# The experts' output biases: from TensorE products to VectorE additions in the node layers

## The reference, cut to what matters

```python
def _L0_ffn_ref(x, Wr, br, W1, b1, ..., Wo, bo):
    ...
    w = jax.nn.softmax(feat @ Wr + br, axis=-1)          # one weight for each node and expert
    h = relu(_bn(einsum('bfd,edh->bfeh', x, W1) + b1))
    h = relu(_bn(einsum('bfeh,ehk->bfek', h, W2) + b2))
    y = jnp.einsum('bfeh,ehd->bfed', h, Wo) + bo         # bo: 8 x 256
    return jnp.einsum('bfed,fe->bfd', y, w)
x = x + _L0_ffn_ref(...)
```

## Time and profile before

| | value |
|---|---|
| median of three runs | 3030.54 us (3022.13 to 3033.51) |
| profiled execution, its own time | 3018.11 us |
| its span, first to last instruction | 3016.4 us |
| PE busy | 2650.0 us (88%) |
| DVE busy | 2043.3 us (68%) |
| ACT busy | 1400.9 us (46%) |
| POOL busy | 1054.2 us (35%) |
| mean granted TensorE clock | 0.948 of full speed |

### The profile page before, as it was taken

How to read it: one execution, slowest core, us unless ns; L and a number is a source line. 1 busy time by engine, 2 the same in 40 slices (tenths; PEclk the granted TensorE clock), 3 DMA queues, 4 the chain that set the end, 5 groups by cost and what they waited for, 6 DMA issues and landing times. The chain is left out here.

```text
span 3016.4 us, 54982 instructions
## 1 busy us (share of the span) xinstructions
PE 2650.0 (88%) x12024; PEld 2076.0 (69%) x12025; DVE 2043.3 (68%) x4092; ACT 1400.9 (46%) x2972; POOL 1054.2 (35%) x1184
## 2 busy tenths in 40 slices
PE   8777787779994999999999999999979977869698
PEld 6545555466552777777768888888858866647587
DVE  6686778868888454553227888888899959955411
ACT  3324332129881443443324444444388948845122
POOL 1676777722110000000006666666500008800043
PEclk9997999989996999999999999999989989989799
DMA  4798999937773000000017777777600131042353
GB/s 163 245 312 272 294 312 303 322 82 229 229 226 134 1 1 9 9 1 9 9 66 227 216 214 214 215 214 214 184 27 33 47 136 50 1 178 88 100 175 127
DMA packets 236592, 443.80 MB, mean 147 GB/s; under 512 B 29017, under 2 KB 128801, under 8 KB 235068
## 3 DMA queue, kind: packets, MB, share of 16 engines
q1 hardware_dynamic: 179518, 261.89, 27.8%
q0 software_dynamic: 56960, 180.47, 19.1%
HBM read 350.56 MB, written 92.69 MB: 147 GB/s over the span
## 5 line engine op out<-in xcount | busy, mean ns | idle before, releaser
L1912 PE MATMUL bank<-sums 128*128 128x256 f32 x2352 | 542.5, 381 | 2.6 <-issue 2.6
L1988 POOL DMA_INDIRECT conv_h<-table_h,conv_ix x392 | 374.2, 955 | 293.2 <-ACT conv_ix L1959 171.6
L1912 PEld LDWEIGHTS bank<-sums 128*128 128x128 f32 x2352 | 434.9, 191 | 54.9 <-issue 3.0
L1719 ACT ACTIVATE area<-bank,nodes_bi,nodes_sc 128x320 f32<-128x320 f32 x320 | 197.5, 617 | 347.2 <-PE bank L1627 347.2
L725 POOL DMA_INDIRECT x<-table_qv,scores_ix x300 | 283.9, 946 | 181.0 <-ACT scores_ix L626 102.7
L1890 DVE SCALAR_TENSOR_TENSOR x<-bank,nodes_w,x 128x256 f32<-128x256 f32 x200 | 96.4, 483 | 296.9 <-PE bank L1636 296.7
L1447 PE MATMUL bank<-attend_pv,x 128*128 128x260 f32 x800 | 220.4, 404 | 26.7 <-POOL attend_pv L1377 24.6
L745 PE MATMUL bank<-sums,area 128*128 x800 | 230.1, 416 | 11.0 <-issue 6.2
L1447 PEld LDWEIGHTS bank<-attend_pv,x 128*128 128x128 f32 x800 | 137.6, 191 | 109.4 <-issue 62.8
L1959 ACT ACTIVATE conv_ix<-src 128x2 int32 x196 | 39.9, 204 | 359.2 <-DVE conv_msg L2009 347.0
L2009 DVE TENSOR_TENSOR conv_msg<-bank,conv_h 128x512 f32<-128x512 f32 x196 | 135.5, 692 | 90.8 <-PE bank L1912 81.4
(11 more groups left out here) (490 smaller groups left out, 5764.6 us busy)
## 6 DMA issues: line engine op xcount, KB each, us to landing
sums<-in_edges SPq DMA_DIRECT2D x196, 384.0 KB, 3.2
x<-edge_v SPq DMA_DIRECT2D x200, 256.0 KB, 3.0
edge_v<-x SPq DMA_DIRECT2D x150, 256.0 KB, 4.7
hidden_rows<-top_wide SPq DMA_DIRECT2D x25, 512.0 KB, 3.4
projected<-spline_hst SPq DMA_DIRECT2D x10, 960.0 KB, 4.4
ball_hT<-projected SPq DMA_DIRECT2D x5, 1920.0 KB, 18.3
top_wd<-in_top_wd SPq DMA_DIRECT2D x8, 1024.0 KB
x<-in_x SPq DMA_DIRECT2D x10, 640.0 KB, 8.8
```

The source lines that it names most:

```text
L1719: nc.scalar.activation((h1, h2)[layer][:, o, hf * CW:(hf + 1) * CW], banks[n % HIDS][:, 0:CW], ACT.Relu, scale=sc[:, layer, e, o:o + 1], b ...
L1912: mm = nc.tensor.matmul(banks[u][:, g * F:(g + 1) * F], m.conv_eT[:, u, g, c], m.conv_w[:, c], start=False, stop=c == EC - 1, skip_group_c ...
L1988: nc.gpsimd.indirect_dma_start(out=h[:, u, g, :], out_offset=None, in_=m.d_h, in_offset=bass.IndirectOffsetOnAxis(ap=ix[:, u * G + g:u * G ...
```

## The change

The bias sum is taken from PE and ACT. The bias rows are loaded onto all 128 partitions in two tiles of 4 x 256 (0.5 MB each), instead of one of 8 x 256. VectorE adds w[k] times bias row k itself: after the sums of expert 0 it does k = 0, after expert 2 k = 1, after 4 k = 2 and 3, after 5 k = 4 and 5, after 6 k = 6 and 7, each with five instructions of 128 x 256. The two PE pieces, ACT's copies, the wait for them and the three additions behind expert 7 go. The semaphore `biased` now counts single additions, and DVE waits on it where the same x is touched next.

```diff
-        bo = st.sb("bo", [XQ, F])
+        near_bo = st.sb("bo", [P, few, F])
+        far_bo = flat[:, NP + 3 * U * F:NP + 3 * U * F + few * F].rearrange("p (e f) -> p e f", f=F)
+        bo = [near_bo[:, e] for e in range(few)] + [far_bo[:, e] for e in range(few)]
+        biases_after = {0: (0, 1), 2: (1, 2), 4: (2, 4), 5: (4, 6), 6: (6, XQ)}
...
-        wT = st.sb("wT", [XQ, CH])
...
                     for k, x in enumerate(("ffn_w1", "ffn_w2", "ffn_wo")):
                         sp.dma_start(W[e][:, k], a[x][e]).then_inc(wload[e], 16)
+                    if e == 0:
+                        sp.dma_start(near_bo[:], a["ffn_bo_near"]).then_inc(bo_loaded, 16)
+                        sp.dma_start(far_bo, a["ffn_bo_far"]).then_inc(bo_loaded, 16)
...
-                        if e == 4 and x is not None:
-                            pe.wait_ge(w_ready, x + 1)
-                            take(kept_w, 2 * x + 2)
-                            for u in range(U):
-                                mm = nc.tensor.matmul(banks[SPARE + u // 3][0:XQ, u % 3 * P:(u % 3 + 1) * P], w[:, x * U + u], m.ident[:],
-                                                      start=True, stop=True)
-                            mm.then_inc(turned_w, 1)
...
-                        if e == 7 and x is not None:
-                            take(biased, x + 1)
-                            for u in range(U):
-                                mm = nc.tensor.matmul(half(u), wT[:, u * P:(u + 1) * P], bo[:], start=True, stop=True)
-                            mm.then_inc(turned_w, 1)
...
-                        if e == 5 and x is not None:
-                            act.wait_ge(turned_w, 2 * x + 1)
-                            for k in range(2):
-                                n = min(3, U - 3 * k) * P
-                                nc.scalar.activation(wT[:, 3 * k * P:3 * k * P + n], banks[SPARE + k][0:XQ, 0:n], ACT.Copy).then_inc(kept_w, 1)
...
                                 dve.wait_ge(summed, (q + 1) * XQ * U)
+                                dve.wait_ge(biased, (q + 1) * XQ * U)
                                 moments(2, m.x[:, tiles(q)])
...
                         if x is not None:
+                            before = [last for at, (_, last) in biases_after.items() if at < e]
+                            if x or before:
+                                dve.wait_ge(biased, (x * XQ + max(before, default=0)) * U)
                             for u in range(U):
...
-                        if e == 7 and x is not None:
-                            dve.wait_ge(turned_w, 2 * x + 2)
-                            dve.wait_ge(summed, (x + 1) * XQ * U)
-                            all_of(nc.vector.tensor_tensor(m.x[:, t], m.x[:, t], bank, ALU.add) for bank, _, t in pairs(x))
-                            dve.sem_inc(biased, 1)
+                        if x is not None and e in biases_after:
+                            if x == 0 and e == 0:
+                                dve.wait_ge(bo_loaded, 32)
+                            dve.wait_ge(summed, (x * XQ + e + 1) * U)
+                            for k in range(*biases_after[e]):
+                                if x or k:
+                                    dve.wait_ge(biased, (x * XQ + k) * U)
+                                for u in range(U):
+                                    xt = m.x[:, x * U + u]
+                                    nc.vector.scalar_tensor_tensor(xt, bo[k], w[:, x * U + u, k:k + 1], xt, ALU.mult, ALU.add).then_inc(biased, 1)
...
-    a["ffn_bo"] = f["L0_ffn_bo"]
+    a["ffn_bo_near"], a["ffn_bo_far"] = _row(f["L0_ffn_bo"][:XQ // 2]), _row(f["L0_ffn_bo"][XQ // 2:])
```

More of the change, by code:

```diff
@@ L1478, in node_layers @@
         br = st.sb("br", [P, XQ])
-        bo = st.sb("bo", [XQ, F])
+        near_bo = st.sb("bo", [P, few, F])
+        far_bo = flat[:, NP + 3 * U * F:NP + 3 * U * F + few * F].rearrange("p (e f) -> p e f", f=F)
+        bo = [near_bo[:, e] for e in range(few)] + [far_bo[:, e] for e in range(few)]
+        biases_after = {0: (0, 1), 2: (1, 2), 4: (2, 4), 5: (4, 6), 6: (6, XQ)}
+        assert steps_at == NP and 3 * U * F + few * F <= STEPS
         raw = st.sb("raw", [P, 2, 5, XQ * FT])
@@ L1513, in node_layers @@
             st.sem(x) for x in ("z_ready", "gate_ready", "var_a", "std_a", "var_b", "std_b", "rows_b", "turned_b", "kept_b"))
-        logits, zs, exps, w_ready, turned_w, kept_w, biased = (
-            st.sem(x) for x in ("logits", "zs", "exps", "w_ready", "turned_w", "kept_w", "biased"))
+        logits, zs, exps, w_ready, bo_loaded, biased = (
+            st.sem(x) for x in ("logits", "zs", "exps", "w_ready", "bo_loaded", "biased"))
         var_c, std_c, rows_c, turned_c, kept_c, h_made, h_kept, h_stored = (
@@ L1546, in _ @@
                 sp.dma_start(m.x[:, tiles(0)], a["x"][0:CH].rearrange("(t p) f -> p t f", p=P)).then_inc(x_back[0], 16)
-                for to, x in ((wr[:], "ffn_wr"), (br[:], "ffn_br"), (bo[:], "ffn_bo"), (m.wskip, "gnn1_wnode")):
+                for to, x in ((wr[:], "ffn_wr"), (br[:], "ffn_br"), (m.wskip, "gnn1_wnode")):
                     sp.dma_start(to, a[x]).then_inc(loaded, 16)
@@ L1572, in _ @@
                 sp.wait_ge(bn_loaded, 32)
-                sp.wait_ge(loaded, 16 * 4)
+                sp.wait_ge(loaded, 16 * 3)
+                sp.wait_ge(bo_loaded, 32)
                 for e in range(XQ):
@@ L1683, in _ @@
                             if p == 0:
-                                pe.wait_ge(loaded, 16 * 4)
+                                pe.wait_ge(loaded, 16 * 3)
                             take(zs, p + 1)
```

## The result

| | before | changed |
|---|---|---|
| median of four runs | 3029.44 us (3022.13 to 3033.51) | 2999.95 us (2998.03 to 3003.98) |
| ratio | | 0.9913, 95% interval 0.9894 to 0.9932 |
| profiled execution, its own time | 3018.11 us | 3003.98 us |
| first VectorE instruction of the stage to first gather behind it | 917.87 to 1578.16: 660.3 us | 920.70 to 1559.69: 639.0 us |

The kernel is 0.87% faster; the interval is 20 to 32 us. The predicted 24.4 us lie in it, and the median in the range. The two profiled executions differ by only 14 us, since outside the stage the changed one lost 7.2 us: 2.8 ahead of it and 4.4 behind it, where the code is the same. Behind the stage two profiles of each kernel took 1438.2 and 1449.1 us before, 1442.6 and 1445.1 us changed: that scatter is as large as half of the gain. So I measure the stage by itself: 21.3 us shorter, 3.1 less than predicted.

A forecast was written before the change was run, and what follows sets the result against it. The prediction took PE alone as full, so time off its order shortens the stage except where VectorE is behind. 6.0 + 10.8 + 4.1 + 3.5 = 24.4 us off the median 3030.54 gave 3006.1 us, range 2996 to 3018.

The forecast's parts named there:

- Turned weights, 6.0 us: On PE after expert 4, the turned weights go: 1.19 us a chunk, 6.0 us over five chunks.
- The change of chunks, 10.8 and 4.1 us: Behind expert 7, VectorE's head 0 starts 3.6 us sooner in three chunks, 10.8 us; into the last, PE gains 4.1 us.
- The stage's end, 3.5 us: Between last sum and moments, the wait for bias products and their addition go: 3.5 us, all passed on.
- the end is not passed on: Rival, chance 0.07: at the stage's end another transfer or the products of zeros end last; gain 20.9 us, 3009.6 us.
- The additions at nothing: VectorE's 200 additions, 0.414 us each, 86 us with waits, fit its idle time ahead of first sums and cost nothing.
- Both rivals with VectorE as the bound: Additions overflow VectorE's gaps: mildly, gain 12.7 us, 3017.8 us, chance 0.10; outright, 40 us slower, 3070 us, chance 0.04.
- the mild rival: At about 0.9 us an addition, VectorE is late ahead of experts 1 and 5, 11.7 us together; 3017.8 us, chance 0.10.
- The loads at nothing: Bias rows in SP's queue grow from 8 KB to 1.05 MB; 3.3 to 7.8 us if not covered, counted as nothing.
- The clock, 1.8 us of the 4.1: The sixteen products behind the bias products go from 6.10 to 4.31 us as the lower clock vanishes: 1.79 us of 4.14.
- the clock stays: Rival, chance 0.15: something else calls for PE's lower clock at the change of chunks; gain 21.7 us, 3008.8 us.

The follow-up runs named there:

- experiment 6: Kernel before, the five bias products with 8 of 128 rows replaced by same-size products with all 128 rows; stage 663.8 us against 660.3.
- experiment 3: Changed kernel with neither engine adding the output biases and no waits for them, bias rows still loaded; stage 633.9 us against 636.2 in experiment 1.
- experiment 4: experiment 1 with five more additions into a scratch row behind each group of five, each waited for; stage 659.6 us, 23.4 us longer.
- experiment 1: Changed kernel with VectorE's wait for the biases riding on a semaphore increment of its own; stage 636.2 us against 639.0, ratio to before 0.9904.
- experiment 5: Kernel before with one more, long satisfied wait in front of the first sum of every expert; stage 664.4 us against 660.3.
- experiment 8: experiment 1 with five unread products of 8 of 128 rows back on PE behind expert 7; stage 640.2 us against 636.2.

## Why the prediction was right, step by step

- **Turned weights, 6.0 us.** From expert 4's first products to expert 5's it was 14.31 us (1138.82 to 1153.13) and is 13.10 (1137.36 to 1150.46): 1.21 us, with 0.07 for the second wait already off it. So the turned weights were worth 1.28 us where I said 1.19, since the output products in front of them had taken 4.50 us instead of 4.41.
- **The change of chunks, 10.8 and 4.1 us.** VectorE's stretch from last to first sum is 3.7 us shorter where I said 3.6, and into the last chunk, from the output products of chunk 3's expert 7 to the first products of the last chunk's expert 1, it was 21.66 us (1430.63 to 1452.29) and is 17.58 (1420.43 to 1438.01): 4.08 us, with two of the new waits already off it. The choice that mattered, to count VectorE's gain and not PE's 4.14 in three of four, held; experiment 6 shows it, where PE only waits longer. The period of a chunk (L1590 to L1590 on POOL before) went from 119.71 to 115.10 us: 4.6 against the forecast 4.8. (Of the four waits in the earlier trace rows three lie behind bias products, as the sum has it, not one.)
- **The stage's end, 3.5 us.** The moments begin 0.04 us behind the last sum instead of 3.63:

```profile
1535.23 0.48 DVE L1884 SCALAR_TENSOR_TENSOR x<-bank,nodes_w,x 128x256 f32<-128x256 f32 x1 [0.43 <-PE bank L1643]
1535.75 1.73 DVE L1772 BATCH_NORM_STATS2 nodes_stats<-x 128x6 f32<-128x256 f32 x5
```

All of it is passed on but for 0.3 us, by rows at a lower clock (7.46 against 6.52 us) against quicker transposes (1.31 against 1.95). The rival "the end is not passed on" fell.
- **The additions at nothing.** 2.07 us for five, as rows 8 had it, and experiment 3. Both rivals with VectorE as the bound fell; experiment 4 shows where they would have begun, and that they could have been dearer than I reckoned, by the lower clock after a wait. (At 0.9 us an addition the group ahead of expert 7, 9.1 against 8.92 us, would have been late too, which the mild rival leaves out.)
- **The loads at nothing.** The first products of expert 1 start 17.6 us behind those of expert 0 in both kernels (962.38 to 979.99, 965.33 to 982.94).
- **What was missing.** I counted the new waits as work in VectorE's free time. The one in front of each first sum is not: it delays that sum by 0.07 to 0.08 us, and PE's third output product waits for it. 32 experts, 2.2 to 2.6 us, a term that the sum put at nothing, shown by experiments 1 and 5 from both sides.
- **The clock, 1.8 us of the 4.1.** The drop behind the bias products is gone, but I took it for certain, and it is a matter of chance: 13 of 20 over five profiles with eight rows there, none of four with full rows, none of 24 with nothing there. One drop behind the router's logits ate the gain in the first profile of the changed kernel; in the second it was kept. So the rival "the clock stays" was wrong on the place and half right on the time.
- **How near the total came, and why.** The pair of profiles without a drop behind the router's logits gives 660.3 - 636.9 = 23.4 us: a little under the forecast, since the waits took 2.4 us and several gains were about 0.1 us larger each time than I said. That the mean of both pairs is 24.1 is in part luck: the second profile of the kernel before is 3.4 us longer than the first, by one drop behind the logits and one spell of lower clock. The whole kernel's medians differ by 29.5 us, 5 more than the stage; nothing in the traces gives those 5 to the change.

## What to carry to other kernels

When an engine's work is moved to another, read the gap at each step, and what both engines wait for at the junction; there the gain is the smaller of the two. A wait that is long satisfied is not free if it stands next to the wait that the critical instruction hangs on: give it another instruction to ride on. And where a ring of two buffers makes the producer wait by a tenth of a us each time, the table of waits does not name it; the distance between starts does. Here a third output bank, taken from the hidden products, took about 7 us off the stage, nearly a third of what the change did.

## What the runs showed of the hardware

- TensorE's clock fell from 2.4 to 1.2 GHz while PE had not been idle, behind products with 8 of 128 rows (13 of 20 times) and behind products with 8 columns (the router's logits, 8 of 48 over twelve profiles), and each time the sixteen products behind took about 1.7 us more. Behind products with all 128 rows of the same size it fell none of 4 times, with nothing in that place none of 24. It also fell after 6 of 9 waits of PE of 2.2 to 2.8 us. The Trainium skill (TensorE: Matmul & The Clock Gate, What's actually happening) ties the lower clock to how busy PE was lately; the runs say that being in use without a gap is not enough.
- Two waits in a row on VectorE put the second into an instruction of 21 ns, and what hangs on it starts 0.07 to 0.08 us later (output products 4.48 us against 4.41, experiments 1 and 5).
- At the stage's end transposes and rows took 5.9 us at a granted clock of 1.00 where PE had been idle for 0.31 us in front of them (experiment 8), and 8.5 us at 0.65 where it had been idle for 1.95 (experiment 1). It is one profile against one.
